# Degree count of a graph layer: one-hot matrices laid out in pairs of columns

## What is computed

```python
deg = segment_sum(ones(E), src, num_segments=n)
perm = argsort(deg + deg_noise, stable=True)
inv = argsort(perm)
y = _mamba(x[perm], ...)          # a recurrence over the nodes in this order
```

## Time and profile before

| | |
|---|---|
| median of 3 runs | 4303.87 us (4298.55 to 4304.12) |
| profiled execution, its own time | 4306.86 us |
| span of the profile | 4305.2 us |
| granted TensorE clock, mean over the span | 0.825 |
| PE busy | 3282.1 us (76%) |
| DVE busy | 2853.0 us (66%) |
| POOL busy | 2353.8 us (55%) |
| ACT busy | 1967.9 us (46%) |

### The profile page before, as it was taken

The page is one execution under the profiler, slowest core; times in us unless marked ns, Lnnn a source line. Parts: engine busy times, 40 slices in busy tenths (PEclk is TensorE's granted clock), DMA queues, the critical chain, the costliest instruction groups (busy, mean ns, idle before and its releaser), DMA issues. The chain is left out here.

```text
span 4305.2 us, 65479 instructions
## 1 busy us (share of the span) xinstructions
PE 3282.1 (76%) x17076; PEld 2489.6 (58%) x17077; DVE 2853.0 (66%) x5471; ACT 1967.9 (46%) x4227; POOL 2353.8 (55%) x2259
## 2 busy tenths in 40 slices
PE   5278778666367878788787887878888488939998
PEld 4177777455255656556565655656565245528887
DVE  4443333689449888888888888888888478721111
ACT  2111111323156666766666576666666265612222
POOL 4442222556766666666666666666666357633444
PEclk8655555667679989989898998988898799969999
DMA  4321112434544444444444444444444623326665
GB/s 150 98 61 44 43 42 65 112 98 108 160 129 114 118 115 114 112 114 110 112 117 109 116 109 118 109 113 113 109 118 105 131 66 101 87 91 145 145 143 109
DMA packets 284402, 460.08 MB, mean 107 GB/s; under 512 B 57687, under 2 KB 203336, under 8 KB 283880
## 3 DMA queue, kind: packets, MB, share of 16 engines
q0 software_dynamic: 121472, 292.57, 27.7%
q1 hardware_dynamic: 162664, 164.81, 13.4%
HBM read 393.75 MB, written 63.44 MB: 106 GB/s over the span
## 5 line engine op out<-in xcount | busy, mean ns | idle before, releaser
L498 POOL DMA_INDIRECT el_g<-table,el_ix x1344 | 1334.4, 993 | 755.3 <-PE fl_ps L616 381.8
L616 PE MATMUL fl_ps<-el_g,el_oh 128*128 128x260 f32 x3520 | 1112.9, 471 | 396.3 <-DVE ACC L551 392.4
L616 PEld LDWEIGHTS fl_ps<-el_g,el_oh 128*128 128x128 f32 x3520 | 797.4, 235 | 745.7 <-issue 576.5
L498 POOL DMA_INDIRECT el_g<-table,eg_src x436 | 453.2, 1040 | 575.4 <-PE fl_ps L616 431.6
L573 ACT CAST el_oh<-fl_pt 128x512 f32<-128x512 bf16 x443 | 256.7, 579 | 934.3 <-PE fl_pt L592 924.4
L1031 DVE TENSOR_TENSOR_SCAN mb_h<-mb_dA,mb_h,mb_dB 128x224 f32<-128x224 f32 x896 | 571.5, 669 | 12.9 <-issue 12.9
L541 DVE TENSOR_TENSOR el_g<-el_g,fl_pw 128x1024 f32<-128x1024 f32 x440 | 532.9, 1211 | 26.5 <-ACT fl_pw L583 26.5
L1268 PE MATMUL fl_py<-mb_hc,ident 128*128 128x448 f32 x896 | 455.0, 592 | 0.1
L559 ACT ACTIVATE el_away<-el_dst,el_less 128x512 bf16<-128x512 bf16 x444 | 319.3, 719 | 166.4 <-DMA el_dst<-dst_rows 103.0
L1158 ACT ACTIVATE mb_dA<-mb_dt,mb_a 128x224 f32<-128x224 f32 x900 | 382.3, 476 | 1.4
L1020 DVE TENSOR_TENSOR mb_dB<-mb_u,fl_pbc 128x448 f32<-128x448 f32 x449 | 274.8, 612 | 114.4 <-PE fl_pbc L1258 112.9
(11 more groups left out here) (298 smaller groups left out, 5219.4 us busy)
## 6 DMA issues: line engine op xcount, KB each, us to landing
el_dst<-dst_rows SPq DMA_DIRECT2D x444, 128.0 KB, 3.4
ex_w<-in_moe_W SPq DMA_DIRECT2D x56, 512.0 KB, 3.6
el_g<-table,el_ix POOLq DMA_INDIRECT x1344
ex_x<-routed_x SPq DMA_DIRECT2D x56, 257.0 KB, 2.8
el_g<-table,eg_src POOLq DMA_INDIRECT x436
mb_x<-sorted_x SPq DMA_DIRECT2D x30, 224.0 KB, 3.5
table<-px_tr POOLq DMA_DIRECT2D x49, 130.0 KB, 2.2
px_x<-in_x SPq DMA_DIRECT2D x49, 128.0 KB, 3.3
```

The source lines that it names most:

```text
L498: pool.indirect_dma_start(out=G[b // GU][:, b % GU * NJ + j, :], out_offset=None, in_=dram["table"], in_offset=bass.IndirectOffsetOnAxis(a ...
L616: mm = nc.tensor.matmul(pS, OH[:, n % (2 * GU), j, :], G[n // GU % 2][:, n % GU * NJ + j, :], start=j == 0, stop=j == NJ - 1)
```

## The change

The one-hot matrices are laid out as 23 pairs of edge columns. Inside a pair, the value runs over 98 (or 64) rows of two elements, one for each edge of the pair. So an element of `HA` is found at [pair, value, edge of the pair]. The weights of one product now lie two elements or 4 bytes apart. `REP` holds each number twice and not 46 times, and is read again for every pair; the comparison reads the two edges of a pair again for every value. The number of instructions, of elements compared and of products is the same, and so is the order of everything.

```diff
-            HI, LO, REP = sb("dg_hif", [P, DC], BF16), sb("dg_lof", [P, DC], BF16), sb("dg_rep", [P, SRC_HI, DB], BF16)
-            HA, HB = sb("dg_ha", [P, 2, SRC_HI, DB], BF16), sb("dg_hb", [P, 2, SRC_LO, DB], BF16)
+            HI, LO, REP = sb("dg_hif", [P, DC], BF16), sb("dg_lof", [P, DC], BF16), sb("dg_rep", [P, SRC_HI, 2], BF16)
+            HA, HB = (sb(f"dg_{n}", [P, 2, DB // 2, v, 2], BF16) for n, v in (("ha", SRC_HI), ("hb", SRC_LO)))
...
-                done(nc.vector.tensor_copy(REP[:], w["iota"][:, 0:SRC_HI].unsqueeze(2).to_broadcast([P, SRC_HI, DB])), wait=False)
+                done(nc.vector.tensor_copy(REP[:], w["iota"][:, 0:SRC_HI].unsqueeze(2).to_broadcast([P, SRC_HI, 2])), wait=False)
...
                 def mark_high(c):
                     if c >= 2:
                         dve.wait_ge(counted, c - 1)
-                    nc.vector.tensor_tensor(HA[:, c % 2], HI[:, c * DB:(c + 1) * DB].unsqueeze(1).to_broadcast([P, SRC_HI, DB]),
-                                            REP[:], ALU.is_equal).then_inc(split_hot, 1)
+                    two = HI[:, c * DB:(c + 1) * DB].rearrange("p (e u) -> p e u", u=2)
+                    nc.vector.tensor_tensor(HA[:, c % 2], two.unsqueeze(2).to_broadcast([P, DB // 2, SRC_HI, 2]),
+                                            REP[:].unsqueeze(1).to_broadcast([P, DB // 2, SRC_HI, 2]), ALU.is_equal
+                                            ).then_inc(split_hot, 1)
 
                 def mark_low(c):
-                    nc.vector.tensor_tensor(HB[:, c % 2], LO[:, c * DB:(c + 1) * DB].unsqueeze(1).to_broadcast([P, SRC_LO, DB]),
-                                            REP[:, 0:SRC_LO, :], ALU.is_equal).then_inc(split_hot, 1)
+                    two = LO[:, c * DB:(c + 1) * DB].rearrange("p (e u) -> p e u", u=2)
+                    nc.vector.tensor_tensor(HB[:, c % 2], two.unsqueeze(2).to_broadcast([P, DB // 2, SRC_LO, 2]),
+                                            REP[:, 0:SRC_LO, :].unsqueeze(1).to_broadcast([P, DB // 2, SRC_LO, 2]), ALU.is_equal
+                                            ).then_inc(split_hot, 1)
...
-                            mm = nc.tensor.matmul(count[:], HA[:, c % 2, :, e], HB[:, c % 2, :, e], start=c == 0 and e == 0,
+                            mm = nc.tensor.matmul(count[:], HA[:, c % 2, e // 2, :, e % 2], HB[:, c % 2, e // 2, :, e % 2], start=c == 0 and e == 0,
                                                   stop=c == ND - 1 and e == DB - 1, skip_group_check=True)
```

## The result

The changed kernel takes 4115.73 us (median of 4 runs, 4106.15 to 4117.69), the kernel before 4303.99 in the same session: a ratio of 0.9561, 95% interval 0.9544 to 0.9578, or 188 us less. The profiled execution is the fastest of the four, 4106.15 us with a span of 4104.5, so that the two profiles lie 201 us apart and not 188.

The account below looks back on a forecast made before the run. A round of marks, `add`, sums and products without overlap was taken to bound the first part. Products 150 us plus clock 30 make 180 off 4303.87, so 4124 us; the 8-in-10 range is 4060 to 4235.

Parts of the forecast that it names:

- The chain: In a plain round of the edge stage's first part, marks, `add`, sums and products follow without overlap: 15.08 us.
- The clock-independent pace as the sign of a read limit: Counting products keep their pace at clocks 0.50 and 0.92, so reading operands 92 bytes apart sets their 180 ns.
- 84 ns a product: Counting products with weights 4 bytes apart fall from 180 to 84 ns at 1.2 GHz; 34 groups give 150 us.
- The clock: TensorE's granted clock in the first part rises from 0.56 to 0.67; sums gain 20 us, products 10.
- rival C: TensorE comes up to 2.4 GHz and stays: round 7.1 us, up to 270 us off, 4034; chance 10%.
- Nothing else late next: In the new 10.7 us round, VectorE's 5.8 us, GpSimd's 5 us of gathers, transfers and ScalarE do not bind.
- VectorE's marks: `mark_high` and `mark_low` keep their pace of nearly two elements per nanosecond, 2.50 and 1.68 us: no change.
- Rival B: Marks fall to one element at a time: `mark_high` 4.84 us, 79 us more in all, total 4203; chance 12%.
- The windows of rows 2: Profile windows taken for the edge stage's first two parts: 526 us at mean clock 0.56, 527 at 0.67.
- Rivals A and D: A: weight loads stay dear, 158 ns, 4250 to 4270, 12%. D: VectorE's marks become the chain, 4338, 4%.
- saves nothing: The change saves nothing in TensorE, the price being in 98 weights, not their distance: about 4304; chance 2%.

Follow-up runs that it names:

- adjacent: Against the changed kernel, weights lie 2 bytes apart and the comparison repeats one edge's number along the row; 4633.80 us, 0.9867 of the kernel before.
- changed_again: The changed kernel itself, unaltered, timed again in a later session; 4557.87 us, 0.9696 of the kernel before.
- marks_last_again: Second timing of the changed kernel with `mark_high` moved behind `add` and `scale`; 4424.77 us, 0.9425 of the kernel before.
- marks_last: The changed kernel with `mark_high` moved behind `add` and `scale`, just before `mark_low`; 4419.04 us, 0.9386 of the kernel before.
- weights_only: Against the kernel before, only `HA` is laid out in pairs, `HB` stays as it was; 4260.39 us against 4301.97, ratio 0.991.

## Why the prediction was right

- *The chain* (marks, `add`, sums, products, nothing overlapping) was read rightly: the steps up to the sums are unchanged to 0.1 us, the sums take 3.8 us at 1.2 GHz and 2.0 at 2.4 as foretold, and the saving of the products came through whole.
- *The clock-independent pace as the sign of a read limit*: right, and now shown by its own experiment, with 1.84 to 1.90 ns for each 16 bytes touched, for loads of 98 weights and for the moving values. The lines of 16 bytes of the Trainium skill ("SBUF — State Buffer", paragraph on cachelines), set beside the prediction's sum but not used in it, agree with this. The "two hits" of the same paragraph of the Trainium skill agree nearly at 1.2 GHz (92 ns at 8 bytes against 83) and not at 2.4 (70 ns at 6 bytes, with over two weights in a line, against 47). The prediction left open whether weights or moving values paid. The answer is both, in parallel.
- *84 ns a product*: 83 at 1.2 GHz. At 2.4 GHz I wrote "no worse" and priced it as 84; it is 48. This term was mis-sized: forecast 150 us and 10 for the clock, measured 286.90 - 101.42 = 185. The working already held a lower price for 2.4 GHz, one tick per weight (41 ns there), and did not use it.
- *The clock*: 0.72 where I took 0.67. The sums gained 20 us by the forecast; by their windows a sum took 128.27 / 34 = 3.77 us before and 113.85 / 35 = 3.25 after, 18 us in 34. Rounds as in rival C (7.1 us) exist, as the one above with 7.20, but they are four of 33: the clock doesn't stay up.
- *Nothing else late next*: wrong by 11 us. The wait for gathers in the fifth round cost 5 (that round kept its 17.1 us from product to product, where others fell by 5 to 8), and the end of the part 6. I had compared GpSimd's 5 us of issue with a mean round, and not asked for the start, where it works off a queue, nor for the end, where its last gathers come after the counts. In the profiles 185 for the products and 18 for the sums, less 11, make 192, which is what the part lost (191.6). That the forecast of 180 came so near the measured 188 is luck in part: a price too high at 2.4 GHz was set off against waits that were not foreseen.
- *VectorE's marks* keep their pace (2.51 and 1.68 us); of the two rules of the Trainium skill weighed there ("Vector Engine (DVE) Microarchitecture Reference", 5.1 and 5.2), the one on inner rows of two elements holds, and the one on runs of adjacent words doesn't bear on a word read again from the same place. Rival B's price (4.84 us, 79 in all) is what `adjacent` pays (4.85, 76), with rows of equal elements.
- *The windows of rows 2*: the 527 us taken for the next part hold the second part and 156 us of the third. The second part alone (743.80 to 1114.30 us) had a clock of 0.69 and not 0.67, which changes nothing in the sum.
- *Rivals A and D* and "saves nothing" are out: at 1.2 GHz weights at 4 bytes cost one tick each (83 ns for 98), and the marks did not grow.

## What to carry to other kernels

When a stream of matmuls keeps its pace while the granted clock doubles, look at how its operands lie: count the 16-byte stretches that a load touches, and find a layout with more of its elements in each. Two to a stretch (8 bytes apart) gave 92 ns at either clock, four 83 and 48. Of the layouts tried, 4 bytes between bf16 values is the one that still lets VectorE compare two at a time. Both operands have to be mended, since the slower read sets the pace. And when an instruction that waits stands ahead of one that another engine needs, move it back: in the last session that brought 133 us where the layout had brought 142, part of it perhaps owed to the late releases told of below.

## What had not been expected of the hardware

In the later sessions an engine that waited for TensorE was often released late. In the first session ScalarE copies (L573) 0.04 us after the last of the four turns ends; in the later one at 398.41, 2.7 us after (395.33 + 0.39). `mark_high` there starts at 398.35, 2.85 us after the products (393.15 + 2.35). The reader of the profile names such a releaser "remote". The first fence is the changed kernel of the first session, the second `changed_again`.

```profile
303.00 0.39 PE L592 MATMUL fl_pt<-el_ident,el_oht 128*128 128x128 bf16 x4
...
303.42 0.59 ACT L573 CAST el_oh<-fl_pt 128x512 f32<-128x512 bf16 x1 [5.25 <-PE fl_pt L592]
```

```profile
393.15 2.35 PE L747 MATMUL dg_count<-dg_hb,dg_ha 128*98 128x64 bf16 x46
...
395.33 0.39 PE L592 MATMUL fl_pt<-el_ident,el_oht 128*128 128x128 bf16 x4
...
398.35 2.51 DVE L693 TENSOR_TENSOR dg_ha<-dg_hif,dg_rep 128x4508 bf16<-128x4508 bf16 x1 [5.51 <-remote]
398.41 0.58 ACT L573 CAST el_oh<-fl_pt 128x512 f32<-128x512 bf16 x1 [5.52 <-remote]
```

Over the first part of `changed_again`, 22 marks of the high values waited for products and started late by 43.5 us in all (2.0 in the median); in the first session's run of the same kernel 22 waited too, and were late by 0.8 us in all. In `marks_last_again` only one such mark waited. So an estimate of the gain of `marks_last` without the late releases of the marks is 133 - 43.5, some 90 us. That the changed kernel gains 142 us in those sessions and not 188 fits this, if the kernel before was released late less often or by less; that isn't shown, as there is no profile of the kernel before from those sessions. What makes the release late was not tried. The record numbers the chip 14 both in the session of `weights_only` (4302 us for the kernel before) and in that of `changed_again` (4700); if the number means the same chip, the lateness isn't a fixed property of one chip, which is what the expectation of `changed_again` had supposed.
